# A mixture-of-experts layer on one core: routing weights moved to GpSimd, low halves and norm sums moved by some steps

## The reference, cut to what matters

```python
def _gemma_mlp(x, gate_w, up_w, down_w):
    g = jnp.einsum('bsh,hi->bsi', x, gate_w)
    u = jnp.einsum('bsh,hi->bsi', x, up_w)
    return jnp.einsum('bsi,ih->bsh', jax.nn.gelu(g, approximate=True) * u, down_w)
rw = jax.nn.softmax(router_logits.astype(jnp.float32), axis=-1)
w, sel = jax.lax.top_k(rw, TOP_K)
w = w / w.sum(axis=-1, keepdims=True)
w = scale * w + (1.0 - scale) * jax.lax.stop_gradient(w)      # scale = 1/12
...                                     # sum over experts of weight * _gemma_mlp
out = out + _gemma_mlp(x, shared_gate, shared_up, shared_down)
x = x + out
```

## Time and profile before

| | before |
|---|---|
| median of the runs | 211.62 us (211.42 to 211.68, three runs) |
| the profiled execution | 211.93 us, of it 210.1 us span |
| TensorE busy | 205.2 us (98%), granted clock 1.0 in every slice |
| VectorE, ScalarE, GpSimd busy | 123.6, 133.8, 117.9 us |
| DMA | 11.70 MB, nearly all in the first 25 us |
| chain that ended last, by engine | TensorE 93%, VectorE 4% |

### The profile page before, as it was taken

One profiled execution on the slowest core, in us unless ns is written; L12 is line 12 of the kernel. 1 busy time (PEld: TensorE's weight loads), 2 busy tenths in 40 slices (PEclk: granted clock), 3 DMA queues, 4 the chain that ended last, 5 costly groups with the idle time before them and its releaser, 6 DMA issues.

```text
span 210.1 us, 6672 instructions
## 1 busy us (share of the span) xinstructions
PE 205.2 (98%) x2695; PEld 165.0 (79%) x2695; DVE 123.6 (59%) x217; ACT 133.8 (64%) x217; POOL 117.9 (56%) x129
## 2 busy tenths in 40 slices
PE   7999999989999999999999999999999999999995
PEld 2444555445444478899999999999999999999995
DVE  2899657977999988554353444434435435344452
ACT  6283767677989997655656656556565565655650
POOL 3023644359548997665565655655656556565562
PEclk9999999999999999999999999999999999999999
DMA  6999600000000000000010010010010010010011
GB/s 196 391 433 434 296 2 0 0 3 0 2 0 5 0 0 3 0 3 5 3 53 3 0 53 3 3 53 0 3 55 3 3 53 0 3 53 4 3 50 53
DMA packets 2813, 11.70 MB, mean 56 GB/s; under 512 B 352, under 2 KB 608, under 8 KB 2400
## 3 DMA queue, kind: packets, MB, share of 16 engines
q1 hardware_dynamic: 2640, 11.01, 13.1%
q10 hardware_dynamic: 144, 0.26, 0.7%
HBM read 9.18 MB, written 2.10 MB: 54 GB/s over the span
## 4 chain that ended last, share of the span: by engine, by line
PE 93%; DVE 4%; issue 1%; ACT 0%; POOL 0%; POOLq 0%
PE o_ps L664 7%; PE g_ps L646 7%; PE u_ps L646 7%; PE o_ps L663 7%; PE u_ps L645 7%; PE g_ps L645 7%; PE u_ps L644 7%; PE g_ps L644 7%; PE o_ps L662 7%; PE u_ps L612 3%; PE g_ps L612 3%; PE g_ps L614 2%; PE o_ps L627 2%; PE o_ps L625 2%; PE o_ps L626 2%; PE g_ps L613 2%
## 5 line engine op out<-in xcount | busy, mean ns | idle before, releaser
L304 POOL TENSOR_TENSOR h<-h 128x512 f16<-128x512 f32 x92 | 109.2, 1194 | 79.2 <-ACT h L340 57.9
L457 DVE SCALAR_TENSOR_TENSOR h<-gel,sk_factor,u_ps 128x512 f32<-128x512 f32 x64 | 47.8, 747 | 68.0 <-PE u_ps L646 39.0
L335 ACT ACTIVATE gel<-g_ps,sk_gate 128x512 f32<-128x512 f32 x64 | 43.9, 687 | 49.8 <-PE g_ps L646 49.8
L340 ACT CAST h<-h 128x512 f16<-128x512 f32 x92 | 56.0, 609 | 3.5 <-DVE h L457 3.5
L645 PE MATMUL g_ps<-x,wsk 128*128 128x128 f16 x256 | 46.2, 219 | 0.0
L646 PE MATMUL g_ps<-x,wsk 128*128 128x128 f16 x256 | 46.2, 219 | 0.0
L645 PE MATMUL u_ps<-x,wsk 128*128 128x128 f16 x256 | 46.2, 219 | 0.0
L646 PE MATMUL u_ps<-x,wsk 128*128 128x128 f16 x256 | 46.2, 219 | 0.0
L644 PE MATMUL u_ps<-x,wsk 128*128 128x128 f16 x256 | 46.2, 219 | 0.0
L644 PE MATMUL g_ps<-x,wsk 128*128 128x128 f16 x256 | 46.2, 219 | 0.0
L663 PE MATMUL o_ps<-h,wsk 128*128 128x128 f16 x256 | 45.9, 219 | 0.0
(11 more groups left out here) (103 smaller groups left out, 310.1 us busy)
## 6 DMA issues: line engine op xcount, KB each, us to landing
wsk<-skills SPq DMA_DIRECT2D x3, 2048.0 KB, 16.1
outT<-xT SPq DMA_DIRECT2D x7, 256.0 KB, 2.0
xT<-xT SPq DMA_DIRECT2D x2, 768.0 KB, 6.3
wsh<-shared SPq DMA_DIRECT2D x3, 256.0 KB, 3.9
xT<-xT ACTq DMA_DIRECT2D x1, 256.0 KB, 3.5
xT<-xT SPq DMA_DIRECT2D x1, 256.0 KB, 4.6
outT<-xT SPq DMA_DIRECT2D x1, 192.0 KB, 2.6
outT<-xT SPq DMA_DIRECT2D x1, 64.0 KB, 1.5
```

Of the source, the lines that this page charges most:

```text
L304: nc.gpsimd.tensor_tensor(hidden_lo(t), hidden_full(t), hidden_hi(t), ALU.subtract).then_inc(lo_ok, 1)
L335: nc.scalar.activation(gel[:, t % NG, :], g_ps[t % 2][:, :], ACT.Gelu_apprx_tanh, scale=scale).then_inc(gelu_ok, 1)
L340: nc.scalar.copy(hidden_hi(t), hidden_full(t)).then_inc(hi_ok, 1)
L457: nc.vector.scalar_tensor_tensor(out=h32[:, t % N32, :], in0=gel[:, t % NG, :], scalar=factor, in1=u_ps[t % 2][:, :], op0=ALU.mult, op1=AL ...
```

## The change

The two routing weights and the four diagonal matrices are made on GpSimd, right behind the first table, where they wait for VectorE's reciprocal (which now follows the probabilities). VectorE makes the low halves of the shared down matrix and of x group 0 ahead of product row 4, not behind it. The self-products of the expert down matrix run in steps 17 to 20 (15 to 18 before). The sum for X_REST goes from step 14 to 15, that for K_UP from 16 to 18, that for K_DOWN from 21 to 24, the masks of K_UP and K_DOWN from 14 to 15 and from 19 to 21, x group 5's high half from step 15 to 16 (its low half from 16 to 17), the X_REST table from 15 to 16 and the expert table from 23 to 26.

```diff
-        K_STEPS = [5, 10, 15]
-        MASK_AT = {3: X_NEXT, 9: K_GATE, 12: X_REST, 14: K_UP, 19: K_DOWN}
-        SPREAD_AT = {4: X_NEXT, 11: K_GATE, 14: X_REST, 16: K_UP, 21: K_DOWN}
+        K_STEPS = [5, 10, 17]
+        MASK_AT = {3: X_NEXT, 9: K_GATE, 12: X_REST, 15: K_UP, 21: K_DOWN}
+        SPREAD_AT = {4: X_NEXT, 11: K_GATE, 15: X_REST, 18: K_UP, 24: K_DOWN}
...
-        TABLE_AT = {4: X_NEXT, 15: X_REST}
-        SKILL_TABLES_AT = 23
+        TABLE_AT = {4: X_NEXT, 16: X_REST}
+        SKILL_TABLES_AT = 26
-        X_AT = {3: 0, 5: 2, 8: 3, 11: 4, 15: 5, 19: 6, 23: 7}
+        X_AT = {3: 0, 5: 2, 8: 3, 11: 4, 16: 5, 19: 6, 23: 7}
...
+            def routing_weights():
+                pool.wait_ge(r_step, 6)
+                nc.gpsimd.tensor_copy(route[:, TOP_K:], top_i[:, 0:TOP_K])
+                nc.gpsimd.tensor_scalar(w_raw[:, :], top_v[:, 0:TOP_K], rpair[:, 0:1], None, ALU.mult).then_inc(r_weight, 1)
+                pool.wait_ge(r_weight, 1)
+                nc.gpsimd.tensor_scalar(w_live[:, :], w_raw[:, :], 1.0 / NUM_MOE_LAYERS, None, ALU.mult)
+                nc.gpsimd.tensor_scalar(w_rest[:, :], w_raw[:, :], 1.0 - 1.0 / NUM_MOE_LAYERS, None, ALU.mult).then_inc(r_weight, 1)
+                pool.wait_ge(r_weight, 2)
+                nc.gpsimd.tensor_tensor(route[:, 0:TOP_K], w_rest[:, :], w_live[:, :], ALU.add).then_inc(r_weight, 1)
+                pool.wait_ge(r_weight, 3)
+                for q in range(2 * TOP_K):
+                    nc.gpsimd.tensor_scalar(spread[:, :, q], ident[0:B, 0:B], route[:, q:q + 1], None, ALU.mult).then_inc(r_spread, 1)
             shared_tables(FIRST)
+            routing_weights()
...
-            def routing_weights():
                 dve.wait_ge(r_step, 5)
-                nc.vector.tensor_copy(route[:, TOP_K:], top_i[:, 0:TOP_K]).then_inc(r_step, 1)
                 nc.vector.reciprocal(rpair[:, :], pair[:, :]).then_inc(r_step, 1)
...
             for t in range(STEPS):
+                if t == C:
+                    shared_low(DOWN, 3)
+                    x_low(0)
                 hidden(t)
-                if t - 1 in X_AT:
+                if t - 1 in X_AT and t != C:
                     x_low(X_AT[t - 1])
...
-                if t == C:
-                    shared_low(DOWN, 3)
...
-                if t == C - 1:
-                    routing_weights()
-                    routing_spread()
```

More of the change, by code:

```diff
@@ L108, in build @@
         w_raw = sb("w_raw", [B, TOP_K], F32)
+        w_rest = sb("w_rest", [B, TOP_K], F32)
         w_live = sb("w_live", [B, TOP_K], F32)
@@ L136, in build @@
         r_step = sem("r_step")
+        r_weight = sem("r_weight")
         r_spread = sem("r_spread")
```

## The result

The changed kernel took 212.26 us (median of 18 runs) against 211.56 us for the kernel before on the same chips: **1.0037 times as long, 95% interval 1.0024 to 1.0051**, or 0.5 to 1.1 us. That is slower, as forecast, and the interval is clear of no change; 212.4 had been predicted, in a range from 210.6 to 213.0. The profiled execution took 212.23 us, of it 210.4 span.

A forecast was written before the change was run, and what follows sets the result against it. TensorE, busy 98% of the span, bounds the kernel, with up(24) set also by VectorE's product row 22. +0.61 for the chain and +0.15 for the slips make +0.76 on 211.62: 212.4 us, range 210.6 to 213.0.

The forecast's parts named there:

- The bound and the mark: TensorE is busy 98%; up(24) at 60.84, set also by VectorE's product row 22, fixes what the kernel gains.
- The prize of 1.6 us: TensorE's late starts before up(24): 0.49 at X_REST's sum, 1.00 at K_DOWN's self-products, 0.1 at up(24).
- The fork: Step 15: X_REST's scales L412 are shut out by subtraction 14, up(24) 0.61 later, or slip past; shut-out case chance 0.52.
- its two branches: L412 shut out: up(24) at 61.45, 0.61 later; L412 slipping past: 60.48, 0.36 gained, all from x high half 5 0.98 earlier.
- Rivals A and B: A: L412 slips past, 211.4, chance 0.25. B: TensorE stays the bound, product row 22 by 58.9, 210.6, chance 0.20.
- The chain's size: Queues of VectorE, ScalarE and GpSimd from step 15 to product row 22, laid end to end: up(24) 0.61 later.
- The slips on the mask: Two GpSimd routing operations slip between VectorE's low halves ahead of mask L393: +0.15 us, bounds 0 and 0.6.
- Rival C: Routing is the loss: a spread running at mask L393 puts 0.6 on TensorE, 212.8 with L412 shut out; within that case's 0.52.
- the time that VectorE wins in step 3: Nine small instructions leave VectorE behind mask L393, where it waits for TensorE again by step 7: worth 0.
- TensorE's new wait at down(12): Step 16: down(12) waits for subtraction 12, which ends at 42.66 whatever TensorE does; 0.4 us come back.
- The other moves at 0: K_DOWN's mask and scales and the later expert table cost 0 at up(24) and after; at most 1.1 if cover is gone.

The follow-up runs named there:

- one wait: Changed kernel with GpSimd's subtraction 14 made to wait until X_REST's scales are made: 211.08 us, 0.9979 of the kernel before.
- the late moves alone: Kernel before with only the later steps of the change, routing still on VectorE: 212.23 us, 1.0019 of the kernel before.
- the two empty writes: Two one-element VectorE writes added in step 6: to the changed kernel 212.33 us; to it with X_REST's scales ahead of expert low half 1, 210.25 us.
- a swap of two instructions: Changed kernel with VectorE's X_REST scales ahead of expert low half 1 in step 15: 210.98 us, 0.9969 of the kernel before.
- one of its moves alone: Kernel before with only K_DOWN's self-products, mask and sum and the expert table moved later: 210.75 us, 0.9944 of the kernel before.
- the four kernels: Changed kernel 212.26 us; kernel before with routing part only 212.16; changed kernel with subtraction 14 waiting for X_REST's scales 211.08, or with those scales first 210.98.

## Why the prediction was right, and where it was not

- **The bound and the mark: right.** The kernel after is slower because up(24) is later, by the wait for product row 22, and from there on it is the same to 0.01 us. The prize of 1.6 us was there to be had.
- **The fork: right, and its size too.** L412 (now L428) was shut out, for 1.14, beginning 0.04 after the subtraction where 0.05 was forecast. Undone by one wait it gave 0.98 back, the difference that the prediction had worked out between its two branches. Rivals A and B, which needed it to slip past or the table to get ahead of expert low half 3, fell with it: L428 took 1.14, and L281 of the table 1.04. The rule from the page SBUF — State Buffer of the Trainium skill (Who interferes with whom), that issue order decides, held here down to 0.04 us.
- **The chain's size: 0.61 forecast, 0.47 measured** with the late moves alone. The hand-overs were too dear: the x high half follows the scales by 0.04 (45.97 to 46.01), not by 0.11, and product row 17 the GELU by 0.03, not 0.07. From there on the laid-out times keep the same distance from the measured ones, to some hundredths.
- **The slips on the mask: 0.15 forecast, 0 measured.** GpSimd's small operations gave way and VectorE's queue did not; the lower bound was the truth. "An operation of 0.3 ends 0.1 later than the short one of 0.2, less the overlap" was the step that failed: the operations do end 0.05 to 0.08 after the low half, but its successor starts ahead of that, unhindered. Rival C fell with it.
- **What was not in it: 0.41 at product row 11.** I held the time that VectorE wins in step 3 to be worth 0. It was worth less than 0, by the place of a boundary in its instruction stream. (VectorE loses eight instructions there, 359 records before and 351 after, not the nine of the prediction.) So the sum came out (+0.76 forecast, +0.70 between the medians, +0.88 in the trace) with one term too large by 0.14, one by 0.15, and one of 0.41 missing. That it came so near is in part luck: only the 0.47 of the fork's chain is there for the reason given, the errors of the other terms nearly cancel.
- **TensorE's new wait at down(12):** 0.4 forecast; 0.87 measured, 0.42 of it from row 11. With the two empty writes the waits view has 0.3 in place of 0.7. The 0.6 that the self-products of K_DOWN still wait in step 17 was not in the forecast; it costs nothing at the mark, which product row 22 sets.
- **The other moves at 0: right.** After the mark no matmul of TensorE up to 100 us has a wait that the profile shows, although product row 31 stood 1.46 us for GpSimd behind the later expert table; TensorE's cover there was enough.

## What to carry to other kernels

Before a norm, a scale or any other tiny VectorE instruction is moved in such a kernel, look at what GpSimd starts on the same event: two instructions released by the same end, one of 0.15 us and one of 1.16, can cost the first a microsecond, and a wait added to the other engine or a swap of two instructions gives it back. A stretch in which TensorE waits for VectorE is read by following VectorE's queue to the wait that it sets last, not by the wait that is seen first: the changed kernel removed one visible wait, shortened the other and lost time, and one of its moves alone would have won 0.5%. And when two kernels differ in a place that neither edit touches, compare one row of each against what releases it.

## What the runs showed of the hardware that was not expected

An engine's instruction count ahead of a place can cost time by itself. VectorE's product row 11 started 0.42 us late in the four kernels in which it is VectorE's 64th instruction (it starts 19.08 after gate(4) in each of them, 18.66 in the kernel before), and on time, at 18.66, once two one-element writes were added 10 us ahead of it; an instruction transfer on q14 moved with it. Three of the six 8 KB transfers that q14 makes in the span follow VectorE's 64th, 192nd and 320th instruction in every trace, so they go with VectorE. Which engines the other three serve, and why the stall is 0.42 and not another length, the runs don't show.

A VectorE scales instruction that reads and writes 128x3 in SBUF is shut out by a running GpSimd subtraction (1.14, 0.56, 0.47 in place of 0.15). One of 128x1 is not: K_DOWN's scales of the kernel before took 0.15 each while a subtraction ran. Nor is the 128x3 one that reads PSUM (L408 at 41.98 in rows 5, 0.15, with a subtraction running from 41.54). Why the 128x1 ones pass, no run tests. And between VectorE's back-to-back low halves GpSimd's 32x2 operations got their turn at no measurable cost to VectorE.
